# Two small-head attentions in one decoder kernel: units of one pair of heads instead of four heads, key tiles weighed in twos, a second copy of the queries, masked columns left out, and one in eight of the maxima taken by ScalarE and GpSimd

## The chip, the cores and the metric

The kernel runs on one core of a Trainium2 chip. The metric is the device time of one execution in microseconds (us). The engines are TensorE (PE, its weight loads PEld), VectorE (DVE), ScalarE (ACT), GpSimd (POOL) and SyncE (SP), which here only starts DMA transfers.

## What is computed

Two decoder layers over x of 1024 tokens by 128, with a context of 6404 by 96. All is float32. The change touches the first two of the six blocks:

```
x = x + self_attention(layernorm(x))             # L0: 16 heads of 8, causal, 1024 queries and keys
x = x + cross_attention(layernorm(x), ctx_768)   # L0: 16 heads of 8, 1024 queries, 6404 keys
x = x + mixture_of_experts(layernorm(x))         # L0
x = x + attention_over_heads(layernorm(x))       # L1, per token, 16 by 16
x = x + cross_attention(layernorm(x), ctx_768)   # L1: 16 heads of 64, 6404 keys
x = x + mixture_of_experts(layernorm(x))         # L1

scores = einsum('bhqd,bhkd->bhqk', q, k) / sqrt(8);  scores = where(causal, scores, -inf)   # self only
probs = softmax(scores, axis=-1);  out = einsum('bhqk,bhkd->bhqd', probs, v)
```

## The kernel before, in words

`decoder` runs the blocks one after another; a barrier of all engines stands between two of them. For the two small-head attentions it calls `project_small_heads` and then `attend_small_heads`.

The projection makes q and k of all heads (`fills` of 512 columns), splits each float32 value into three bfloat16 parts (ACT takes the first and second part, DVE the rest and the third) and writes the parts to DRAM through a ring of three (`RING`, semaphores `out`, L198 waits for it). After the fills, TensorE makes the values, four tiles of 128 keys to a PSUM bank, and DVE copies them into `Vall` (L222).

The attention loads from DRAM so that a head's score is one bfloat16 product over 64 rows: six row blocks of 8 hold the six products of parts that matter (`PRODUCTS`, `ROWS`), and one row (`ROW`) is one in the keys and minus the query's maximum in the queries. Two heads (s = 0, 1) lie side by side, on rows 0 to 63 and 64 to 127. A group is four heads: two such pairs, a = 0, 1.

Work goes in units n of one group by one half of the queries (512): 8 units for each attention (`UNITS`). In a unit there is

- a maximum item ("m") for each chunk of 512 keys, pair and tile of 128 queries. TensorE makes the scores query by key in two PSUM banks, one for each head (`take`, L421; on the diagonal it adds a mask, L427), and DVE reduces each bank to 128 maxima (L544). Cross-attention: 13 chunks x 2 pairs x 4 tiles = 104 items and 208 reductions in a unit.
- after a unit's last item, one reduction over chunks (L548), a turn ("t") of the maxima to rows: 16 products of one column with the identity for each pair (L438), and ACT's `negate`, which writes minus the maxima into the row `ROW` of `Qst` (L506).
- steps j, one for each tile of 128 keys (51 in a cross unit, 4 or 8 in a self unit): `score(j, 0)` and `score(j, 1)` on banks 0 to 3 (L460; with the causal mask over all 512 columns, L465), ACT's exponentials of 128 x 1024 (L525), and `weigh(j)`: four products side by side in column groups of 32, one for each head, into bank 4 (L479).
- ACT copies the sums out (L513), TensorE turns them ("o", L445), DVE divides (L556, L560).

The order is written down before the kernel is built (`plan`): the maxima of unit n+1 are spread over the steps of unit n, and `AHEAD` items (4 self, 10 cross) beyond it. TensorE's order in step j is: the two scores, the first half of the step's items, `weigh(j-1)`, the second half. Items take their banks in turn from three, 5 to 7 (`bank`), two banks each: so an item waits (L398) until the item before it has had its first bank reduced, and the item before that its second. No step starts before all items of unit 0 and `AHEAD` more are through (`first`), on the same three banks.

SP loads all parts. From group 2 on it waits until the group two before is scored. The query tile is single in `Qst`, and the row for minus the maxima stands in it: before the maxima of group g+1 POOL must clear that row again (L372, `row_cleared`), which comes after `spare` in POOL's order. `spare` is `clear_cross` during the self attention: POOL clears the tiles of the later cross attention (L1539, L1542, L1543) and sets their ones rows (L1534).

Of the kernel before, what the change touches and what calls it, by code (L numbers as in the profile page):

```python
# [19 lines left out]
P = 128  # L20
# [16 lines left out]
ROWS = (0, 8, 16, 24, 40, 48)  # L37
ROW = 32
# [99 lines left out]
def project_small_heads(nc, name, m, PS, keysT, krows, nkeys, wk, wv, qsrcT, wq, bq, kparts, qparts, Vall,  # L138
                        spare=None):
# [3 lines left out]
    ntiles = -(-nkeys // P)  # L143
    RING = 3
    fills = [("q", f * HALF, HALF) for f in range(HALVES)]
    fills += [("k", c, min(HALF, ntiles * P - c)) for c in range(0, ntiles * P, HALF)]
    with ExitStack() as stack:
        s = Mem(nc, stack, name)
        rest = s.sb("rest", [P, 2, HALF])
        parts = s.sb("parts", [P, RING, PARTS, HALF], BF16)  # L150
        biased = s.sb("biased", [P, 2, HALF])
        filled, biased_ok, part1, rest1 = s.sem("filled"), s.sem("biased_ok"), s.sem("part1"), s.sem("rest1")
        part2, part3 = s.sem("part2"), s.sem("part3")
        out = [s.sem(f"out{b}") for b in range(RING)]
        v_filled, v_copied, ones_set = s.sem("v_filled"), s.sem("v_copied"), s.sem("ones_set")
        vbanks = -(-ntiles // 4)
        block = stack.enter_context(nc.Block())

        @block.tensor
        def _(pe):  # L160
            for n, (kind, c, w) in enumerate(fills):
                if n >= 2:
                    pe.wait_ge(rest1, n - 1)
                if kind == "q":
                    i = pe.matmul(PS[:, n % 2, 0:w], wq, qsrcT[0:P, c:c + w], start=True, stop=True)
                else:
                    i = pe.matmul(PS[:, n % 2, 0:w], wk, keysT[0:krows, c:c + w], start=True, stop=True)
                i.then_inc(filled, 1)
            for t in range(ntiles):
                b = t // 4  # L170
                if t % 4 == 0 and b >= 4:
                    pe.wait_ge(v_copied, b - 3)
                i = pe.matmul(PS[:, 4 + b % 4, (t % 4) * P:(t % 4 + 1) * P], keysT[0:krows, t * P:(t + 1) * P], wv,
                              start=True, stop=True)
                if t % 4 == 3 or t == ntiles - 1:
                    i.then_inc(v_filled, 1)

        @block.scalar
        def _(act):
            def second(n):  # L180
                w = fills[n][2]
# [1533 lines left out]
```

## Time and profile before

| | |
|---|---|
| time, median of 3 runs | 4343.45 us (4342.44 to 4351.64) |
| the profiled execution | 4342.88 us, its span 4341.1 us |
| PE busy | 3724.0 us (86%) |
| DVE busy | 2818.0 us (65%) |
| ACT busy | 1998.2 us (46%) |
| POOL busy | 1868.0 us (43%) |
| self attention, first item to last division | 44.66 to 298.0 us |
| cross-attention, first item to last division | 382.78 to 1601.9 us |

PE busy is the sum over the whole program. The two attentions of the change are the first 1602 us; the blocks after them, from 1602 us on, are not touched. A row of the timeline gives start, length, engine, line, operation, the tiles, and in brackets the idle time before it and what ended it. Rows of the same kind that follow each other closely are one row with xN; consecutive instructions of an engine can overlap, so the length of such a row is less than the sum.

### The profile page before, as it was taken

How to read it: one execution, taken by the hardware profiler on the slowest of the kernel's cores; microseconds unless marked ns; L12 is line 12 of the kernel's file. 1: busy time of each engine (PE TensorE's matmuls, PEld its weight loads, DVE VectorE, ACT ScalarE, POOL GpSimd, SP SyncE). 2: the span in 40 equal slices, each digit the busy share in tenths (PEclk: the TensorE clock that was granted, in tenths of full speed). 3: DMA queues.
4: the chain of work that ended last, by engine and by line, in shares of the span. 5: the costliest groups of instructions: out<-in, count | busy, mean ns of one | idle time of the engine just before them, and what ended most of it. 6: DMA issues, size and time to landing. Idle time of an engine off the chain costs nothing. (4 is left out here: it accounts for less than half of the span.)

```text
span 4341.1 us, 56316 instructions
## 1 busy us (share of the span) xinstructions
PE 3724.0 (86%) x21560; PEld 1506.4 (35%) x21560; DVE 2818.0 (65%) x4320; ACT 1998.2 (46%) x2265; POOL 1868.0 (43%) x760
## 2 busy tenths in 40 slices
PE   5775478888888889885899999999999999999799
PEld 1222112221122224332344444444444444444343
DVE  4436899999999702276666676666667666675222
ACT  2441067777777872250244444444444444444312
POOL 3500000000000000050488887888888788889700
PEclk7885599999999988795899999999999999999889
DMA  2004000200100000060011010101101010011110
GB/s 62 15 1 107 0 1 1 28 1 1 28 1 1 1 18 25 6 247 11 15 28 29 25 30 27 29 27 29 29 25 31 28 29 27 27 29 32 34 41 5
DMA packets 71842, 122.88 MB, mean 28 GB/s; under 512 B 9741, under 2 KB 25691, under 8 KB 70907
## 3 DMA queue, kind: packets, MB, share of 16 engines
q1 hardware_dynamic: 71580, 119.28, 9.8%
q8 instruction: 177, 2.90, 0.3%
q14 instruction: 85, 0.70, 0.1%
HBM read 84.62 MB, written 34.64 MB: 27 GB/s over the span
## 5 line engine op out<-in xcount | busy, mean ns | idle before, releaser
L967 POOL TENSOR_TENSOR att_total<-att_total,att_prob 128x1024 f32<-128x1024 f32 x608 | 1569.9, 2582 | 333.9 <-ACT att_prob L1162 282.3
L1179 DVE TENSOR_REDUCE att_top_piece<-PS 128x1 f32<-128x512 f32 (+1 forms) x1664 | 1036.7, 665 | 364.4 <-PE PS L1028 354.5
L544 DVE TENSOR_REDUCE att_top_piece<-PS 128x1 f32<-128x512 f32 (+4 forms) x1856 | 1128.5, 654 | 217.2 <-PE PS L421 107.0
L1162 ACT ACTIVATE att_prob<-PS 128x1024 f32<-128x1024 f32 x816 | 791.6, 1022 | 1005.6 <-PE PS L1086 1001.8
L525 ACT ACTIVATE att_prob<-PS 128x1024 f32<-128x1024 f32 x912 | 880.4, 1021 | 358.1 <-PE PS L460 293.9
L1099 PE MATMUL PS<-att_prob,att_vals 128*64 128x512 f32 x3264 | 791.9, 605 | 3.7 <-issue 2.9
L421 PE MATMUL PS<-cross_Kstack,cross_Qstack 64*128 64x512 bf16 (+1 forms) x1664 | 343.2, 403 | 275.0 <-DVE att_top_piece L544 255.7
L1028 PE MATMUL PS<-att_k_hi,att_q_hi 64*128 64x512 f32 (+1 forms) x1664 | 396.7, 469 | 87.1 <-DVE att_top_piece L1179 86.5
L361 POOL COPY cross_Vst<-cross_Vall 128x1836 f32<-128x1836 f32 x4 | 7.6, 1898 | 1036.4 <-PE PS L479 989.9
L479 PE MATMUL PS<-att_prob,cross_Vst 128*32 128x512 f32 x3264 | 437.9, 605 | 0.6 <-ACT att_prob L525 0.4
L421 PEld LDWEIGHTS PS<-cross_Kstack,cross_Qstack 64*128 64x128 bf16 x1664 | 94.9, 94 | 785.1 <-DVE att_top_piece L544 749.9
L1073 PE MATMUL PS<-att_q_hi,att_k_hi 64*128 64x512 f32 x1632 | 327.9, 397 | 1.1 <-ACT att_prob L1162 1.1
L1028 PEld LDWEIGHTS PS<-att_k_hi,att_q_hi 64*128 64x128 f32 x1664 | 167.4, 190 | 463.4 <-issue 273.9
L1073 PE MATMUL PS<-att_q_hi,att_k_lo 64*128 64x512 f32 x1632 | 323.5, 391 | 0.0
L1073 PE MATMUL PS<-att_q_lo,att_k_hi 64*128 64x512 f32 x1632 | 323.0, 390 | 0.0
L1099 PEld LDWEIGHTS PS<-att_prob,att_vals 128*64 128x64 f32 x3264 | 197.5, 136 | 335.8 <-issue 328.7
L460 PE MATMUL PS<-cross_Qstack,cross_Kstack 64*128 64x512 bf16 x1632 | 256.0, 379 | 11.1 <-ACT att_prob L525 6.6
L1229 DVE TENSOR_TENSOR k_xn<-k_xn,att_prob 128x1024 f32<-128x1024 f32 x160 | 209.5, 1309 | 58.4 <-ACT att_prob L1162 58.4
L1086 PE MATMUL PS<-att_minus_max,att_key_ones 32*128 32x512 f32 x1632 | 207.1, 496 | 0.0
L1196 DVE TENSOR_TENSOR att_k_lo<-PS,att_k_hi 128x512 fp32r<-128x512 f32 (+1 forms) x104 | 70.8, 681 | 206.8 <-ACT att_k_hi L1144 206.8
L1073 PEld LDWEIGHTS PS<-att_q_hi,att_k_hi 64*128 64x128 f32 x1632 | 155.2, 185 | 47.6 <-ACT att_prob L1162 23.1
L1073 PEld LDWEIGHTS PS<-att_q_hi,att_k_lo 64*128 64x128 f32 x1632 | 155.1, 185 | 34.9
(240 smaller groups left out, 2870.5 us busy)
## 6 DMA issues: line engine op xcount, KB each, us to landing
att_vals<-values SPq DMA_DIRECT2D x192, 256.0 KB, 2.6
values<-mla_stage SPq DMA_DIRECT2D x24, 1024.0 KB, 4.1
f_w<-in_f_w SPq DMA_DIRECT2D x40, 256.0 KB, 4.5
cross_Kstack<-kparts SPq DMA_DIRECT2D x36, 204.0 KB
kparts<-proj_parts SPq DMA_DIRECT2D x42, 128.0 KB
att_vals<-values SPq DMA_DIRECT2D x16, 192.0 KB, 2.3
k_ctxT<-in_ctxT SPq DMA_DIRECT2D x1, 2448.0 KB
cross_Kstack<-kparts SPq DMA_DIRECT2D x36, 64.0 KB
```

Of the source, the lines that this page charges most:

```text
L421: i = pe.matmul(PS[:, bank(p + s), 0:w], Qst[rows, g % 2, a, at:at + P], Kst[rows, g % 2, a, c * HALF:c * HALF + w], start=True, stop=True ...
L460: i = pe.matmul(PS[:, 2 * (e % 2) + s, :], Kst[rows, g % 2, a, kt * P:(kt + 1) * P], Qst[rows, g % 2, a, cols(n)], start=True, stop=not ma ...
L479: i = pe.matmul(PS[32 * k:32 * k + 32, PV, :], Vst[:, kt, k, :], prob[:, j % RING, k, :], start=(kt == 0), stop=(kt == tiles_of(n) - 1), t ...
L525: act.activation(prob[:, j % RING, 2 * a:2 * a + 2, :].rearrange("p a b -> p (a b)"), PSf[:, e % 2 * 2 * HALF:(e % 2 * 2 + 2) * HALF], ACT ...
L544: dve.tensor_reduce(top_piece[:, n % 2, k, c:c + 1], PS[:, bank(p + s), 0:w], AX, ALU.max).then_inc(dve_freed, 1)
L967: pool.tensor_tensor(so_far, so_far, prob[0:rows, j % RING, :, :], ALU.add).then_inc(summed, 1)
L1028: ins = pe.matmul(PS[:, bank(at + s), 0:w], q_hi[strip(s), n % QBUFS, qt * P:(qt + 1) * P], k_hi[strip(s), p % 2, c * HALF:c * HALF + w], ...
L1073: pe.matmul(PS[:, b + s, :], k[strip(s), p % 2, keys], q[strip(s), n % QBUFS, :], start=start, stop=False, tile_position=(s * DH2, 0))
L1099: i = pe.matmul(PS[strip(s), PV, :], vals[:, value_slot(n, kt // 4), kt % 4, strip(s)], prob[:, j % RING, s, :], start=(kt == 0), stop=(kt ...
L1162: act.activation(prob[:, j % RING, :, :].rearrange("p a b -> p (a b)"), PSf[:, b:b + 2 * HALF], ACT.Exp, scale=scale).then_inc(exped, 1)
L1179: dve.tensor_reduce(top_piece[:, n % 2, s * QT + qt, c:c + 1], PS[:, bank(at + s), 0:w], AX, ALU.max).then_inc(dve_freed, 1)
L1229: dve.tensor_tensor(total_dve, total_dve, now, ALU.add).then_inc(dve_summed, 1)
```

## The change

`project_small_heads` and `attend_small_heads` become one function, `small_heads`, with one block of engines.

- A unit is one pair of heads by one half of the queries: 16 units. A cross unit has 52 items.
- A step is two tiles of keys (26 steps in a cross unit, the last one with one tile; 2 or 4 in a self unit). `weigh` puts the two heads of the first tile in column groups 0 and 1 and of the second in 2 and 3; the two halves of the sums are added when they are turned ("o"), by a product with `fold`, two identities on top of each other.
- `ROW` stays 32, but the last two row blocks lie behind it, so that a strip is 49 rows and not 64.
- Queries are held twice: `Qm` for the maxima, whose row 32 stays zero, and `Qs` for the scores, where ACT writes minus the maxima. L372's clearing and `row_cleared` are gone; `clear_cross` is shorter and sets rows as float32 words, two bfloat16 each.
- "t" is four transposes of a 128 x 128 tile whose columns 32 and 96 hold the maxima.
- In the causal attention, scores, exponentials and `weigh` leave out the columns before the diagonal (`first_column`), and the mask is added to 128 columns (256 in one tile of every other unit), not 512.
- In the cross-attention the second bank of every item with qt = 3 (of chunks 0 to 10: 11 of a unit's 104 banks) is copied by ACT into `run` or a ring of three `stage` tiles, and POOL joins it to `run` as run + max(stage - run, 0) in three instructions. DVE reduces `run` once a unit.
- `first` uses all eight banks. The projection has rings of four, makes a values bank after each keys fill, ACT and DVE copy these by turns, and ACT starts the load of the first piece of keys while SP loads the queries.

```diff
@@ items, bank by bank @@
+    def is_copied(item, s):
+        return not causal and item[0] == "m" and s == 1 and item[3] == QT - 1 and item[2] < NCH - 2
+        need = 2 if item[0] == "m" else 1
+        if k < len(first):
+            mine = [(at + i) % 8 for i in range(need)]
+        else:
+            mine = [SIDE + (at + i) % BANKS for i in range(need)]
...
+        waits[item] = [user[b] for b in mine if b in user]
@@ weigh @@
-                for k in range(GROUP):
-                    i = pe.matmul(PS[32 * k:32 * k + 32, PV, :], Vst[:, kt, k, :], prob[:, j % RING, k, :],
-                                  start=(kt == 0), stop=(kt == tiles_of(n) - 1), tile_position=(0, 32 * k))
+                for par, kt in enumerate(kts):
+                    lo = first_column(n, kt, par, i)
+                    for s in range(2):
+                        r = 32 * (2 * par + s)
+                        ins = pe.matmul(PS[r:r + 32, PV, lo:HALF], Vst[:, u % 2, kt, s, :],
+                                        prob[:, j % RING, par, s, lo:HALF], start=(i == 0),
+                                        stop=(kt + 2 >= tiles_of(n)), tile_position=(0, r))
@@ turn of the maxima, turn of the sums @@
-                        for qt in range(QT):
-                            k = (a * QT + qt) * 2 + s
-                            i = pe.matmul(PS[r:r + 1, bank(p), qt * P:(qt + 1) * P], top[:, n % 2, k:k + 1],
-                                          ident[:, :], start=True, stop=True, tile_position=(0, r))
+                    for qt in range(QT):
+                        i = pe.transpose(PS[:, banks[item][0], qt * P:(qt + 1) * P], top[:, qt, :], ident[:, :])
...
+                        i = pe.matmul(PS[:, banks[item][0], qt * 64:(qt + 1) * 64], heads_out[:, qt * P:(qt + 1) * P],
+                                      fold, start=True, stop=True)
@@ the mask of the scores @@
-                        i = pe.matmul(PS[:, 2 * (e % 2) + s, :], identb[:, :],
-                                      by_key[:, HALF - P - first_col:2 * HALF - P - first_col], start=False, stop=True)
+                        i = pe.matmul(PS[:, 2 * (e % 2) + s, lo:diagonal + P], identb[:, :],
+                                      by_key[:, HALF - P - diagonal + lo:HALF], start=False, stop=True,
+                                      skip_group_check=True)
@@ the copied maxima: ACT, POOL, DVE @@
+                    act.activation(to, PS[:, banks[item][1], :], ACT.Copy).then_inc(tile_copied, 1)
...
+                    pool.wait_ge(tile_copied, copy_number[item] + 1)
+                    pool.wait_ge(tile_joined, i)
+                    at, now = run[:, :], stage[:, i % STAGE, :]
+                    pool.tensor_tensor(now, now, at, ALU.subtract).then_inc(tile_ahead, 1)
+                    pool.wait_ge(tile_ahead, 2 * i + 1)
+                    pool.tensor_scalar(now, now, 0.0, None, ALU.max).then_inc(tile_ahead, 1)
+                    pool.wait_ge(tile_ahead, 2 * i + 2)
+                    pool.tensor_tensor(at, at, now, ALU.add).then_inc(tile_joined, 1)
...
+                        dve.wait_ge(tile_joined, joined_up_to[n])
+                        dve.tensor_reduce(top_piece[:, n % 2, 2 * QT - 1, 0:1], run[:, :], AX,
+                                          ALU.max).then_inc(run_taken, 1)
@@ clear_cross, before @@
-                if g == 0:
-                    pool.memset(Kcross[:, :, :, :], 0.0).then_inc(cross_cleared, 1)
...
-                    ones_rows(pool, Kcross, 0, NCTX, cross_cleared)
@@ attend_small_heads, before: the row in the queries @@
-                        pool.memset(Qst[r:r + 1, (g + 1) % 2, :, :], 0.0).then_inc(row_cleared, 1)
...
-                                pe.wait_ge(row_cleared, 2 * (g - 1))
```

The first place is TensorE in the cross-attention, in the steps of the first unit. Kernel before (L460 scores, L421 item, L479 weigh):

```order
L460 MATMUL PS<-cross_Qstack,cross_Kstack 128x512 x4
L421 MATMUL PS<-cross_Kstack,cross_Qstack 128x512 x2
L479 MATMUL PS<-att_prob,cross_Vst 32x512 x4
L421 MATMUL PS<-cross_Kstack,cross_Qstack 128x512 x2
L460 MATMUL PS<-cross_Qstack,cross_Kstack 128x512 x4
L421 MATMUL PS<-cross_Kstack,cross_Qstack 128x512 x2
L479 MATMUL PS<-att_prob,cross_Vst 32x512 x4
L421 MATMUL PS<-cross_Kstack,cross_Qstack 128x512 x2
```

The same engine and place in the changed kernel (L489 scores, L450 item, L515 weigh):

```order
L489 MATMUL PS<-cross_Qscore,cross_Kstack 128x512 x4
L450 MATMUL PS<-cross_Kstack,cross_Qmax 128x512 x2
L515 MATMUL PS<-att_prob,cross_Vst 32x512 x4
L450 MATMUL PS<-cross_Kstack,cross_Qmax 128x512 x2
L489 MATMUL PS<-cross_Qscore,cross_Kstack 128x512 x4
L450 MATMUL PS<-cross_Kstack,cross_Qmax 128x512 x2
L515 MATMUL PS<-att_prob,cross_Vst 32x512 x4
L450 MATMUL PS<-cross_Kstack,cross_Qmax 128x512 x2
```

Nothing has moved inside a step: the same four kinds in the same order with the same counts.

The second place is ACT in a later cross unit of the changed kernel, about the end of one unit (L605 exponentials, L572 minus the maxima, L586 copies for POOL); before, the exponentials of a unit stood there with four L506 and one L513 among them:

```order
L605 ACTIVATE att_prob<-PS 128x1024 x4
L586 ACTIVATE att_stage<-PS 128x512
L605 ACTIVATE att_prob<-PS 128x1024 x10
L572 ACTIVATE cross_Qscore<-PS 1x512 x2
L605 ACTIVATE att_prob<-PS 128x1024 x2
L586 ACTIVATE att_run<-PS 128x512
```

A copy stands behind every fourth exponential, which is every second step, and none in four of the steps.

The third place is POOL during the self attention. Kernel before (row writes of the later cross tile and the clearing that TensorE waits for):

```order
L1534 MEMSET cross_Kstack 1x4x6404
L372 MEMSET self_Qstack 1x2048 x2
```

Changed kernel:

```order
L374 COPY self_Vst<-self_Vall 128x16x9
L1648 MEMSET cross_Kstack 1x4x3202
L1648 MEMSET cross_Kstack 1x4x62
L374 COPY self_Vst<-self_Vall 128x16x9
```

The clearing behind the long write is gone, and the write has half the elements.

## Rows read from the trace of the kernel before

**Rows 1.** Windows: length, busy time (instructions) of each engine, PEclk, DMA share, GB/s.
```profile
44.60:298.80 254.20, 192.23 (x1312) 59.47 (x1312) 103.53 (x216) 116.32 (x136) 72.87 (x12) 0.86 0.03 10
690.90:962.90 272.00, 224.91 (x1714) 55.38 (x1712) 258.86 (x423) 203.61 (x215) 5.50 (x3) 1.00 0.08 12
2150.00:4000.00 1850.00, 1806.17 (x10970) 848.99 (x10970) 1253.05 (x1885) 807.12 (x884) 1531.12 (x603) 1.00 0.10 28
```

**Rows 2.** Timeline, one step in the middle of the cross-attention.
```profile
903.68 0.39 PE L421 MATMUL PS<-cross_Kstack,cross_Qstack 64*128 64x512 bf16 x2 [0.45 <-DVE att_top_piece L544]
904.00 1.06 PE L479 MATMUL PS<-att_prob,cross_Vst 128*32 128x512 f32 x8
905.00 0.39 PE L421 MATMUL PS<-cross_Kstack,cross_Qstack 64*128 64x512 bf16 x2
905.65 1.94 ACT L525 ACTIVATE att_prob<-PS 128x1024 f32<-128x1024 f32 x2 [0.65 <-PE PS L460]
906.27 0.39 PE L421 MATMUL PS<-cross_Kstack,cross_Qstack 64*128 64x512 bf16 x2 [0.45 <-DVE att_top_piece L544]
```

**Rows 3.** Groups by line and form, 540 to 1508 us: busy, mean ns, idle before.
```profile
L544 DVE TENSOR_REDUCE att_top_piece<-PS 128x1 f32<-128x512 f32 x1343 | 858.1, 686 | 29.9 <-PE PS L421 18.7
```

**Rows 4.** Timeline, two items one step apart where the last chunk has 260 keys.
```profile
805.61 0.29 PE L421 MATMUL PS<-cross_Kstack,cross_Qstack 64*128 64x260 bf16 x2
...
807.72 0.29 PE L421 MATMUL PS<-cross_Kstack,cross_Qstack 64*128 64x260 bf16 x2
```

**Rows 5.** Timeline, the stretch before the first step of the cross-attention.
```profile
382.78 0.61 PE L421 MATMUL PS<-cross_Kstack,cross_Qstack 64*128 64x512 bf16 x2 [16.35 <-DMA cross_Kstack<-kparts]
...
417.61 1.29 DVE L544 TENSOR_REDUCE att_top_piece<-PS 128x1 f32<-128x512 f32 x2 [0.20 <-PE PS L421]
...
552.39 1.94 ACT L525 ACTIVATE att_prob<-PS 128x1024 f32<-128x1024 f32 x2 [12.58 <-PE PS L460]
```

**Rows 6.** Timeline of ACT and TensorE at unit ends; then the copies one unit apart.
```profile
675.95 2.03 PE L438 MATMUL PS<-k_ident,att_top 128*1 128x128 f32 x29
...
690.91 0.60 ACT L513 ACTIVATE att_heads_out<-PS 128x512 f32<-128x512 f32 x1
...
826.89 0.60 ACT L513 ACTIVATE att_heads_out<-PS 128x512 f32<-128x512 f32 x1
```

**Rows 7.** Timeline, two steps of the last cross unit, and the end.
```profile
1593.56 1.06 PE L479 MATMUL PS<-att_prob,cross_Vst 128*32 128x512 f32 x8
...
1595.40 1.07 PE L479 MATMUL PS<-att_prob,cross_Vst 128*32 128x512 f32 x8
...
1602.91 1.64 PE L586 MATMUL PS<-k_ident,k_O 128*128 128x128 f32 x8 [1.59 <-PEq L55]
```

**Rows 8.** Timeline, the first loads of the cross-attention.
```profile
367.78 4.75 SPq L382 DMA_DIRECT2D cross_Qstack<-qparts  x12
```

**Rows 9.** Timeline, POOL and TensorE in the self attention, two places.
```profile
134.28 21.44 POOL L1534 MEMSET cross_Kstack<- 1x25616 bf16 x1
...
159.64 0.29 PE L421 MATMUL PS<-self_Kstack,self_Qstack 64*128 64x128 bf16 x2 [17.32 <-issue]
...
220.53 0.29 PE L421 MATMUL PS<-self_Kstack,self_Qstack 64*128 64x128 bf16 x2 [8.27 <-issue]
```

**Rows 10.** Timeline, turn of the sums and the two masks in the self attention.
```profile
171.15 0.29 PE L427 MATMUL PS<-self_by_query,k_identb 128*128 128x128 bf16 x2
...
173.53 0.66 PE L445 MATMUL PS<-k_ident,att_heads_out 128*128 128x128 f32 x4
...
176.52 0.60 PE L465 MATMUL PS<-self_by_key,k_identb 128*128 128x512 bf16 x2
```

**Rows 11.** Groups by form: POOL over the whole span.
```profile
L951 POOL TENSOR_TENSOR k_O<-k_O,att_sums 128x512 f32<-128x512 f32 x16 | 21.5, 1347 | 6.3 <-DVE att_sums L1209 6.3
L361 POOL COPY cross_Vst<-cross_Vall 128x1836 f32<-128x1836 f32 x4 | 7.6, 1898 | 1036.4 <-PE PS L479 989.9 <-POOLq L55 46.5
```

**Rows 12.** Groups by form, 2150 to 4000 us.
```profile
L1179 DVE TENSOR_REDUCE att_top_piece<-PS 128x1 f32<-128x512 f32 x1387 | 892.1, 685 | 284.5 <-PE PS L1028 275.2
```

More of the change, by code:

```diff
@@ L375, in _ @@
[L375 to L391 removed]
+            pool.memset(Vall[:, 0:NT, :, DH:DH + 1], 1.0).then_inc(v_ones, 1)
@@ new lines, in _ @@
+            pool.wait_ge(v_ones, 3 if nkeys % P else 1)
+            pool.wait_ge(v_by_act, VBANKS // 2)
+            pool.wait_ge(v_by_dve, VBANKS - VBANKS // 2)
+            for u in range(2):
+                stage_values(u)
+            for item in first:
+                join(item)
+            for j in range(STEPS):
+                n, i = steps[j][0], j - base[steps[j][0]]
+                for item in plan[j]:
+                    join(item)
+                u = n // HALVES
+                if n % HALVES == 0 and i == 1 and 1 <= u and u + 1 < PAIRS:
+                    stage_values(u + 1)
+                    if spare is not None:
+                        pool.wait_ge(staged, u + 2)
+                        spare(pool, u)
@@ L403, in take @@
                 if item[0] == "m":
[L404 to L414 removed]
+                    c, qt, w = item[2:]
@@ L485, in _ @@
             for j in range(STEPS):
-                score(j, 0)
-                score(j, 1)
+                for par in range(len(steps[j][1])):
+                    score(j, par)
                 items = plan[j]
@@ new lines, in _, with side @@
+            second(len(fills) - 1)
+            for n in range(HALVES, min(len(fills), HALVES + PIECE)):
+                act.wait_ge(out[n % OUT], 16 * PARTS * (n // OUT + 1))
+            load(act, Kst, kparts, 0, piece(0), 0, first_loaded[0])
+            def side(item):
+                if item[0] == "t":
+                    n = item[1]
+                    g, a = place(n)
+                    act.wait_ge(top_turned, n + 1)
+                    for s in range(2):
+                        r = 64 * s + ROW
+                        act.activation(Qs[r:r + 1, g % 2, a, cols(n)], PS[r:r + 1, banks[item][0], :], ACT.Copy,
+                                       scale=-1.0).then_inc(negated, 1)
+                elif item in copy_number:
+                    n, c = item[1:3]
+                    act.wait_ge(max_scored, maximum_number[item] + 1)
+                    if c == 0:
+                        if n >= 1:
+                            act.wait_ge(run_taken, n)
+                        to = run[:, :]
+                    else:
+                        i = join_number[item]
+                        if i >= STAGE:
+                            act.wait_ge(tile_joined, i - STAGE + 1)
+                        to = stage[:, i % STAGE, :]
+                    act.activation(to, PS[:, banks[item][1], :], ACT.Copy).then_inc(tile_copied, 1)
```

686 lines of the change are left out of this document (360 added, 326 removed).

## The prediction

> **What bounds the kernel now.** Both attentions of the change lie in the first 1602 us; nothing after them is touched, so the sum is made over this stretch. I read the windows first, to see which engine is full, then the timeline of one step, to see which wait ends last in it, then the stretches before the first step and after the last.
>
> In the middle of the cross-attention no engine is full: of 272.0 us TensorE is busy 224.9, DVE 258.9, ACT 203.6, at a granted clock of 1.00, which is 2.4 GHz [rows 1]. DVE at 95% looks like the bound. The step says something else. Steps follow each other in 906.27 - 903.68 = 2.59 us [rows 2]. Two reductions of one item take 1.29 us as a row, so the second starts 1.29 - 0.69 = 0.60 after the first [rows 3, 5]; four at that spacing are 2.40 us, less than 2.59. The path that closes on itself is this one [rows 2, 3]: item a issues (903.68), `weigh` 0.32 later (904.00), item b 1.00 later, when `weigh` has streamed (905.00), b's products end 0.39 later (905.39), DVE reduces b's first bank in 0.69 (906.08), and the next a, which needs just that bank, issues at 906.27. The 0.19 left over are two handovers. 0.32 + 1.00 + 0.39 + 0.69 + 0.19 = 2.59. The second bank of an item is not on it. Where the items are 260 keys wide the same path gives 807.72 - 805.61 = 2.11 us [rows 4].
>
> A unit of 51 steps takes 826.89 - 690.91 = 136.0 us [rows 6]; 47 x 2.59 + 4 x 2.11 = 130.2 of it are steps, 5.8 are the turns at its end (the 32 turn products are two runs like that of 2.03 us in rows 6, and one run of 0.66 for the sums, rows 10, with what waits behind them).
>
> Before the first step stand 104 items and ten of the lead on three banks, at half the clock (an item's products 0.61, not 0.39): DVE waits 0.20 for TensorE at each, 1.49 us an item; 552.39 - 382.78 = 169.6 us pass from the first item to the first exponential [rows 5]. The last unit has no maxima and goes at 1595.40 - 1593.56 = 1.84 us a step, near ACT's two exponentials of 1.94 as one row [rows 2, 7]; less the 1.00 of `weigh` that leaves 0.84 for two scores.
>
> In the self attention TensorE is busy 192 of 254.2 us at a clock of 0.86 [rows 1]. In two places it stands 17.3 and 8.3 us with nothing that the profile names [rows 9]; there it waits for POOL's clearing of row 32, which is queued behind a write of 21.4 us.
>
> **The change, part by part.**
>
> *Cross, before the first step.* 52 items on eight banks. DVE no longer waits 0.20: 41 items of two reductions at 1.20 (spacing 0.60) to 1.29, I take 1.25; 11 of one at 0.65; the run tile 0.65; four of these items are narrow, -1.5: 58 us. The turn at half clock and the reduction over chunks: 2. Then ten items of the lead, two with one reduction only: 12, since the scores need the banks of the last three items. 1 for handovers. 73 us against 169.6: **-97** (bounds -87, if each of 52 items keeps the 0.20, to -103).
>
> *Cross, the steps.* TensorE's order inside a step is the same as before (the first pair of order lists), and an item still waits for the first bank of the item before. The banks taken off DVE are second banks, which are not on the path. So a wide step keeps 2.59, a narrow one 2.11: 24 x 2.59 + 2 x 2.11 = 66.4 us a unit. At its end are one turn of four transposes (I take the 0.66 of four transposes in rows 10 for it) in place of two runs of 2.0, and one of the sums; each also shifts the banks by one, so that the next item waits for a second bank too, 0.6. Two times 0.66, half of the two 0.6, ACT's two row writes: 2.0, between 1.3 and the 2.9 of half of 5.8. 68.4 us a unit, where half a unit before was 68.0: nothing won.
> ACT gets 11 copies of 0.60 a unit [rows 6]: 1.94 + 0.60 = 2.54 in every second step, below 2.59 and just covered; if that cover went, a step of 2.6 to 2.8 would cost up to 2 us a unit.
> POOL gets ten joins a unit. The two-input instruction of this size is 1.35 [rows 11]; a one-input one lies between 1.90 x 512 / 1836 = 0.53 (the copy) and 1.35. A join is 3.2 to 4.1, with handovers 3.5 to 4.4, in two steps of 5.18 us: covered. DVE waits for the last join only five items (three steps) after its tile: covered too. Both at nothing.
> Units 0 to 13: 14 x 68.4 = 958, with 2.5 for the first, which starts at the low clock (552.39 to 690.91 is 138.5 before). Unit 14 has only 42 items left to take: 16 steps of 2.59 and 10 of some 2.2 (two scores 0.84, `weigh` 1.0, one item 0.3): 64. Unit 15 has none: 51 tiles x 0.92 = 47. The end 3 as now. Together 1075, against 1602.91 - 552.39 = 1050.5: **+24**. That a half unit in which DVE idles is replaced by one in which it works takes back a quarter of what the start gives.
>
> *Cross, projection and first loads.* SP's query load (4.75 us to issue) and the first keys after it now start on two queues at once: -4 of the 15.0 us from 367.78 to the first item [rows 5, 8]. The values between the fills, a ring of four and one barrier less: at least -1, at most -14 (the 13 value banks now come after the fills). Together -5 to -18; I take **-12**.
>
> *Self attention.* The two gaps go: 17.3 + 8.3 = 25.6 [rows 9]; `staged` is then all that TensorE needs of POOL, and its long write is half as many elements (some 10.7 us by 21.4 / 2, if the cost goes by elements) with a pair of units of over 20 us to hide in; cover gone, it would cost some of those 25.6. The mask over 512 columns, 0.53 to 0.60 for a pair of products, becomes one over 128, 0.22 to 0.29 [rows 10]: 64 x 0.32 = 20. Sixteen turns of 0.66 for sixteen runs of 2.0, minus eight more turns of sums at 0.66: 16 x 1.35 - 5 = 16. Left-out columns (a quarter of `weigh` and scores on the diagonal tiles, 0.2 each on 32 pairs): 6. Four items fewer in `first` on eight banks: 5; the smaller last unit: 3. Sum 75.6; since part of mask and columns lies beside the reductions that an item waits for (four items to a step where the next unit is the long one), I take two thirds of 20 + 6: 67. Loads on two queues and one barrier less: 5. **-72**, bounds -45 (only the gaps, the turns and a little) and -90.
>
> Sum: -97 + 24 - 12 - 72 = -157. 4342.9 - 157 = 4186, and the profiled execution is 0.6 us under the median: **4186 us**.
>
> **A rule against this change.** The reductions cost 685 ns with POOL busy 1531 of 1850 us, and 686 ns where POOL idles [rows 1, 3, 12]: no contention to be seen. The Trainium skill (Perfetto Trace Analysis, Optimizing Scalar/DVE Operations) warns that GpSimd and DVE share an SBUF read port, so that moving work between the two might not help; it also says, in SBUF — State Buffer, Who interferes with whom, that `tensor_reduce` on trn2 never contends. By the first sentence the joins would slow the reductions, by the second and by the rows they would not; the rows decide.
>
> **Rivals.**
> 1. *DVE is the bound in the steps, and the copies relieve it.* For it: 95% busy. Then two steps have seven reductions in place of eight; TensorE's own work, 0.84 + 1.00 + two items of 0.32 and at least 0.21 (512 columns at 2.4 GHz), 2.37 to 2.48 a step, comes next: 24 x 2.39 + 2 x 2.11 + 2 = 63.6, with its waits 64.4, a unit 4 shorter. 14 x 4 = 56 less: 4130 us. Against it: the path above has 2.59 with nothing left for it.
> 2. *ACT or POOL becomes the bound in the steps*, ACT through its copies behind two exponentials, or POOL with 1.9 us an instruction: two steps become 6.0, 11 x 0.8 = 9 a unit, +140: 4326 us. For it: ACT's cover is only 0.05. Against it: rows 11, and score banks for two exponentials ahead.
> 3. *Slower: the joins block DVE.* POOL's 4 us of SBUF work in every two steps would hold the reductions. The point from which the change loses is 157 / (11 x 16) = 0.9 us in two steps; if blocked for all of it, two steps take some 8.8, +3.6 x 176 = 630: over 4800 us. Against it: rows 3 and 12.
> 4. *The self attention gives only its low bound* and the start of the projection too: 4186 + 27 + 7 = 4220 us.
>
> **How the numbers follow.** My forecast 0.60; the first rival 0.18; the second 0.07; the third 0.03; the fourth 0.12. The range: below, the first rival with another 20 from self and projection, 4110; above, the fourth with 2 us more in each of 15 units, 4250. Slower than before by over 0.2% (8.7 us, which is about what a measurement can tell) is only the third, 0.03; within 0.2% 0.02; faster 0.95.
>
> **What would show it.** The first exponential of the cross-attention some 73 us after its first item. Copies out of the sums 68.4 us apart, and steps of 2.59 with TensorE still waiting 0.4 for DVE's first bank; if they are 64 apart, the path was not the bound; if TensorE or ACT waits there for POOL, the second rival. The reductions still 0.69 each; at 1 us or more, the third. No gap over 3 us on TensorE in the self attention, and that stage some 185 us from its first item. What would make the forecast wrong most: a step whose path is no longer through b's first bank, because ACT's copies delay the exponentials by more than the 0.05.

## The result, and the profile after

The changed kernel takes 4201.2 us (median of 4 runs, 4196.86 to 4204.58), the kernel before 4342.94 us (4 runs, 4340.66 to 4351.64). The ratio is 0.967, with a 95% interval of 0.965 to 0.969: 142 us faster. The forecast was 4186 us in a range of 4110 to 4250. Its mechanism in the cross-attention held, to 0.6 us a unit; the self attention gave less than half of what was forecast.

The profiled execution took 4204.58 us with a span of 4202.4 us, 138.7 us less than the span before. The stretches, with the difference from before:

| stretch | before | after | difference | predicted |
|---|---|---|---|---|
| self attention: first turn of `O` behind it, on the clock of the run | 298.8 | 268.4 | -30.4 | -72 |
| projection and loads, to the first cross item | 84.0 | 62.9 | -21.1 | -12 |
| cross, first item to first exponential | 169.6 | 66.9 | -102.7 | -97 |
| cross, first exponential to the first turn of `O` | 1050.5 | 1068.7 | +18.2 | +24 |
| all later blocks | 2738.2 | 2735.5 | -2.7 | 0 |

The timeline of the changed kernel has the edges of the cross-attention. Columns are start, length, engine, line, operation, tiles, idle before and who ended it; these rows answer to [rows 5, 7]:

```profile
331.30 1.89 PE L450 MATMUL PS<-cross_Kstack,cross_Qmax 49*128 49x512 bf16 x8 [18.86 <-DMA cross_Qmax<-qparts]
...
398.20 1.02 ACT L605 ACTIVATE att_prob<-PS 128x1024 f32<-128x1024 f32 x1 [4.27 <-PE PS L489]
...
1466.93 1.48 PE L696 MATMUL PS<-k_ident,k_O 128*128 128x128 f32 x8 [1.51 <-PEq L58]
```

A step in the middle of the cross-attention, which answers to [rows 2]:

```profile
703.20 1.06 PE L515 MATMUL PS<-att_prob,cross_Vst 128*32 128x512 f32 x8
...
704.20 0.39 PE L450 MATMUL PS<-cross_Kstack,cross_Qmax 49*128 49x512 bf16 x2
...
704.63 0.60 ACT L586 ACTIVATE att_stage<-PS 128x512 f32<-128x512 f32 x1 [0.44 <-PE PS L450]
705.12 1.94 ACT L605 ACTIVATE att_prob<-PS 128x1024 f32<-128x1024 f32 x2
705.30 1.27 POOL L382 TENSOR_TENSOR att_stage<-att_stage,att_run 128x512 f32<-128x512 f32 x1 [0.98 <-ACT att_stage L586]
...
705.47 0.39 PE L450 MATMUL PS<-cross_Kstack,cross_Qmax 49*128 49x512 bf16 x2 [0.45 <-DVE att_top_piece L647]
...
705.79 1.07 PE L515 MATMUL PS<-att_prob,cross_Vst 128*32 128x512 f32 x8
...
706.66 1.48 POOL L384 TENSOR_SCALAR att_stage<-att_stage 128x512 f32<-128x512 f32 x1
```

From `weigh` at 703.20 to `weigh` at 705.79 are 2.59 us, as before, and TensorE still stands 0.45 us before item a for DVE, although in this step ACT copies a bank (704.63) and POOL joins it. The copies of the sums, which answer to [rows 6]:

```profile
469.37 0.60 ACT L592 ACTIVATE att_heads_out<-PS 128x512 f32<-128x512 f32 x1
...
537.07 0.60 ACT L592 ACTIVATE att_heads_out<-PS 128x512 f32<-128x512 f32 x1
...
604.78 0.60 ACT L592 ACTIVATE att_heads_out<-PS 128x512 f32<-128x512 f32 x1
```

67.7 us a unit here and 67.8 in the later ones; half a unit before was 68.0. The windows of the changed kernel (length, busy time and instructions of PE, PEld, DVE, ACT and POOL, granted clock, DMA share, GB/s) answer to [rows 1]:

```profile
43.20:267.00 223.80, 186.74 (x1216) 73.33 (x1216) 106.53 (x239) 101.50 (x144) 33.17 (x13) 0.74 0.06 17
...
147.00:155.00 8.00, 5.40 (x42) 1.98 (x42) 6.27 (x12) 3.52 (x6) 3.92 (x3) 0.89 0.00 0
155.00:163.00 8.00, 7.26 (x42) 3.19 (x38) 3.40 (x9) 2.63 (x4) 0.00 (x0) 0.50 0.01 2
...
537.10:604.80 67.70, 57.24 (x424) 14.21 (x422) 59.02 (x98) 56.23 (x66) 41.34 (x31) 1.00 0.00 1
```

In the cross-attention the clock is 1.00 as before. In the self attention it is 0.74, where it was 0.86, and it is here that the forecast failed. Groups by form over 469 to 1350 us answer to [rows 3, 11]; the copies and the joins are there for the first time:

```profile
L647 DVE TENSOR_REDUCE att_top_piece<-PS 128x1 f32<-128x512 f32 x1106 | 716.5, 686 | 105.1 <-PE PS L450 94.8
...
L384 POOL TENSOR_SCALAR att_stage<-att_stage 128x512 f32<-128x512 f32 x130 | 192.9, 1484 | 11.4
L386 POOL TENSOR_TENSOR att_run<-att_run,att_stage 128x512 f32<-128x512 f32 x130 | 166.0, 1277 | 10.9
L382 POOL TENSOR_TENSOR att_stage<-att_stage,att_run 128x512 f32<-128x512 f32 x130 | 165.7, 1275 | 328.3 <-ACT att_stage L586 328.3
L586 ACT ACTIVATE att_stage<-PS 128x512 f32<-128x512 f32 x130 | 77.6, 597 | 45.4 <-PE PS L450 45.4
```

The reductions took 686 ns while POOL worked 41.3 of 67.7 us beside them. That agrees with the Trainium skill (SBUF — State Buffer, Who interferes with whom), by which `tensor_reduce` on trn2 never contends with GpSimd. These reductions read PSUM; the one in each unit that reads `run` in SBUF took 675 ns.

### The profile page after: what moved, and what is told of

Read it like the earlier page. It is cut to its first block and busy times, and to the rows that moved or that the text cites. A ratio compares the mean times of both kernels' runs of the same rounds, so it can differ in the third digit from the quotient of the medians.

```text
span 4202.4 us, 57008 instructions
## 1 busy us (share of the span) xinstructions
PE 3694.7 (88%) x21368; PEld 1514.6 (36%) x21368; DVE 2718.1 (65%) x4201; ACT 2076.1 (49%) x2464; POOL 2452.6 (58%) x1245
## 5 line engine op out<-in xcount | busy, mean ns | idle before, releaser
L1272 ACT ACTIVATE att_prob<-PS 128x1024 f32<-128x1024 f32 x816 | 791.6, 1022 | 1004.5 <-PE PS L1196 1000.7
L647 DVE TENSOR_REDUCE att_top_piece<-PS 128x1 f32<-128x512 f32 (+4 forms) x1680 | 1020.5, 650 | 237.3 <-PE PS L450 141.7
L605 ACT ACTIVATE att_prob<-PS 128x1024 f32<-128x1024 f32 (+2 forms) x912 | 863.8, 1004 | 188.3 <-PE PS L489 151.8
L450 PE MATMUL PS<-cross_Kstack,cross_Qmax 49*128 49x512 bf16 (+1 forms) x1664 | 330.2, 391 | 187.8 <-DVE att_top_piece L647 165.8
L515 PE MATMUL PS<-att_prob,cross_Vst 128*32 128x512 f32 x3264 | 443.7, 606 | 0.5 <-ACT att_prob L605 0.2
L382 POOL TENSOR_TENSOR att_stage<-att_stage,att_run 128x512 f32<-128x512 f32 x160 | 203.8, 1274 | 401.1 <-ACT att_stage L586 399.8
L450 PEld LDWEIGHTS PS<-cross_Kstack,cross_Qmax 49*128 49x128 bf16 x1664 | 92.8, 93 | 686.7 <-DVE att_top_piece L647 517.3
L489 PE MATMUL PS<-cross_Qscore,cross_Kstack 49*128 49x512 bf16 x1632 | 258.4, 380 | 19.5 <-ACT att_prob L605 13.2
L384 POOL TENSOR_SCALAR att_stage<-att_stage 128x512 f32<-128x512 f32 x160 | 237.4, 1484 | 14.0
L386 POOL TENSOR_TENSOR att_run<-att_run,att_stage 128x512 f32<-128x512 f32 x160 | 204.1, 1276 | 13.4
```

What stands on the lines that cost most here:

```text
L384: pool.tensor_scalar(now, now, 0.0, None, ALU.max).then_inc(tile_ahead, 1)
L450: i = pe.matmul(PS[:, banks[item][s], 0:w], Qm[rows, g % 2, a, at:at + P], Kst[rows, g % 2, a, c * HALF:c * HALF + w], start=True, stop=Tr ...
L489: i = pe.matmul(PS[:, 2 * (e % 2) + s, lo:HALF], Kst[rows, g % 2, a, kt * P:(kt + 1) * P], Qs[rows, g % 2, a, n % HALVES * HALF + lo:(n % ...
L515: ins = pe.matmul(PS[r:r + 32, PV, lo:HALF], Vst[:, u % 2, kt, s, :], prob[:, j % RING, par, s, lo:HALF], start=(i == 0), stop=(kt + 2 >= ...
L605: act.activation(prob[:, j % RING, par, :, lo:HALF], PS[:, 2 * (e % 2):2 * (e % 2) + 2, lo:HALF], ACT.Exp, scale=scale).then_inc(exped, 1)
L647: dve.tensor_reduce(top_piece[:, n % 2, s * QT + qt, c:c + 1], PS[:, banks[item][s], 0:w], AX, ALU.max).then_inc(dve_freed, 1)
```

## The experiments

Unit times below are distances of two copies of the sums; kernel times are medians of four runs.

**1. No copies.** `is_copied` gives False, and DVE's reduction of `run` goes.

```diff
-        return not causal and item[0] == "m" and s == 1 and item[3] == QT - 1 and item[2] < NCH - 2
+        return False
```

> DVE takes all maxima of the cross-attention itself; ACT's 12 copies and POOL's 11 joins of a unit go. By the path theory the banks given away are second banks and off the path: copies of the sums stay 67.8 us apart, only the stretch before the first exponential grows, by 11 reductions of 0.6, 66.9 -> 73 us; kernel 4201 -> 4205 to 4212 us. By the rival (DVE is the bound, the copies relieve it) a unit grows by some 4 us, kernel some 4260 us. If the copies only cost, it is a little faster than 4201.

Measured: 4214.1 us (ratio to before 0.970, 0.969 to 0.972), 2 us above the expected range. Units of 67.7 us in the middle; first item 333.35, first exponential 407.42, so 74.1 us in place of 66.9. DVE is busy 64.8 us of a unit, not 59.0, and the unit is no longer. The copies pay only ahead of the first step.

**2. Half of the first bank, or half of the second.** Both relieve DVE by the same amount.

```diff
-dve.tensor_reduce(..., PS[:, banks[item][s], 0:w], AX,
+dve.tensor_reduce(..., PS[:, banks[item][s], 0:(HALF // 2 if not causal and s == 0 and w == HALF else w)], AX,
```

(`s == 1` for the second bank. Both kernels leave keys out of the maxima.)

> In the cross-attention DVE reduces only the left 256 columns of the first bank of each wide item (the right half of these keys is left out of the maxima). By the path theory (item a, weigh, item b, DVE's first bank, next a) a step loses about half of the 0.69 us reduction, some 0.3 us, until TensorE's own 2.0 us or ACT's 1.9 us a step are near: step 2.59 -> 2.3 to 2.4, copies of the sums 67.8 -> 60 to 62.5 us apart, kernel 4201 -> about 4100 to 4125 us. If DVE's total (59.0 of 67.7 us a unit) were the bound, the gain would be the same here and in the kernel with the second banks halved.

> The same cut of 256 columns, but in the second bank of each wide item (the right half of these keys is left out of its maxima). DVE is relieved as much as with the first banks halved. By the path theory nothing comes of it: copies of the sums stay 67.8 us apart, kernel 4201 us within 8. If DVE's total were the bound, the unit would fall to 60 to 63 us and the kernel to some 4110 us.

Measured: first bank 4108.4 us (0.946, 0.945 to 0.948), second bank 4198.2 us (0.967, 0.965 to 0.968). The timeline of the kernel with half a first bank, then of the one with half a second:

```profile
523.27 0.61 ACT L592 ACTIVATE att_heads_out<-PS 128x512 f32<-128x512 f32 x1
...
585.10 0.61 ACT L592 ACTIVATE att_heads_out<-PS 128x512 f32<-128x512 f32 x1
```

```profile
532.44 0.60 ACT L592 ACTIVATE att_heads_out<-PS 128x512 f32<-128x512 f32 x1
...
599.78 0.60 ACT L592 ACTIVATE att_heads_out<-PS 128x512 f32<-128x512 f32 x1
```

61.8 us a unit against 67.3; the changed kernel takes 67.7 there. The halved reduction takes 425 ns in place of 686; 24 wide steps by 0.26 are 6.3 us a unit, and 5.9 came. The second banks gave 0.3 to 0.4 for the same relief. The step goes through b's first bank, and DVE's total is not its bound.

**3. Single waits, and another order.** In the cross-attention each of an item's two products waits for its own bank and tells DVE of itself; then the items are also laid around the scores. The edit is shortened:

```diff
-                for before in waits[item]:
-                    wait_freed(*before)
+                        if not causal and banks[item][s] in user_before[item]:
+                            wait_freed(*user_before[item][banks[item][s]])
@@ second kernel: order in a cross step @@
-                score, score, item a, weigh, item b
+                score, a's first product, score, a's second and b's first, weigh, b's second
```

> In the cross-attention each of an item's two products waits for its own bank alone and tells DVE of itself, in place of one wait and one signal for both; order unchanged. By the path theory the product whose bank is free goes earlier, and DVE starts on b's first bank before the second product ends: 0.05 to 0.1 us a step, 20 to 40 us of the kernel, 4161 to 4181 us. Rival: the two products then no longer stream side by side (each half of TensorE's rows), an item takes 0.43 us longer and the twice as many waits cost some 0.05 each: 4201 to 4240 us.

> As the kernel with single waits, and the order on TensorE inside a cross step is changed too: score, first product of item a, score, a's second product and b's first, weigh, b's second product; before, score, score, item a, weigh, item b. By the path theory three of the four banks of a step are then refilled while weigh waits or runs, and DVE never waits for the end of weigh with more than one bank empty: step 2.59 -> 2.40 to 2.48 us, unit 67.8 -> 63 to 65, kernel 4140 to 4165 us. Rival: the scores are parted by products that wait for DVE, so the second exponential is late, ACT becomes part of the path, and the step grows to 2.6 to 2.9: 4200 to 4320 us.

Measured: 4173.9 us (0.961, 0.960 to 0.962) with units of 65.5 us, and 4158.0 us (0.957, 0.956 to 0.959) with units of 64.8. Both beat the changed kernel. With the spread order TensorE is busy 62.7 of 64.8 us:

```profile
529.10:593.90 64.80, 62.69 (x424) 15.02 (x422) 57.31 (x98) 56.45 (x66) 41.36 (x32) 1.00 0.01 1
```

The same 424 products had taken 57.2 us. In its timeline one product stands where the pair had stood, and is as long as the pair (0.39 us in the step above):

```profile
699.66 0.39 PE L454 MATMUL PS<-cross_Kstack,cross_Qmax 49*128 49x512 bf16 x1
...
700.97 0.39 PE L454 MATMUL PS<-cross_Kstack,cross_Qmax 49*128 49x512 bf16 x1
```

So a part of the won wait seems to be spent again on products that no longer stream side by side. This is a reading of the busy records, whose ends are modelled; no run tests it by itself.

**4. The mask over all columns.** In the self attention only.

```diff
-                        i = pe.matmul(PS[:, 2 * (e % 2) + s, lo:diagonal + P], identb[:, :],
-                                      by_key[:, HALF - P - diagonal + lo:HALF], start=False, stop=True,
+                        i = pe.matmul(PS[:, 2 * (e % 2) + s, lo:HALF], identb[:, :],
+                                      by_key[:, HALF - P - diagonal + lo:2 * HALF - P - diagonal], start=False, stop=True,
```

> In the self attention the mask product of a score runs again to column 512 in place of 128 columns; the result is the same. It adds 64 times some 0.3 us of TensorE work at full clock where the scores begin left of the diagonal's end. Theory 1: the narrow masks won less than their work because TensorE's clock in this stage is granted at 0.74 only, and more work raises it: self stage 223.8 us within 5, clock above 0.74. Theory 2: the work is simply on the path: the stage grows by 10 to 20 us at the same clock, kernel 4212 to 4220 us.

Measured: 4211.8 us (0.970, 0.969 to 0.972). From the first item to the last copy of the sums 228.5 us against 221.9, +6.6, at a clock of 0.77 against 0.74. This lies between the two theories. The edit also adds less than the 64 times 0.3 us of its expectation: the columns left of `lo` stay out, so a masked tile gets 192 more columns on average and not 384. At full clock two units are busy 19.6 us on TensorE in place of 18.3 (rows under experiment 5), an estimated 10 us in the eight pairs of the stage, and 6.6 came.

**5. The self attention's items twice.** The same two products are issued again into the same banks.

> In the self attention each item's two products are issued twice into the same banks (result unchanged): 15 us more of TensorE work at 2.4 GHz, 31 us at 1.2 GHz. Theory 1 (the low clock is what the stage lost, and it comes from TensorE being too little busy): granted clock 0.74 -> 0.85 or more, the stage 223.8 us -> 205 to 225 though work was added. Theory 2 (clock does not follow work, or the added work is on the path): 235 to 255 us at a clock near 0.74.

Measured: 4216.7 us (0.972, 0.969 to 0.974). The stage takes 224.2 us against 221.9, with 192 more products (1400 instructions for 1208) but not more time on TensorE:

```profile
42.49:266.70 224.21, 187.22 (x1400) 69.55 (x1400) 106.52 (x238) 100.56 (x143) 33.20 (x13) 0.84 0.06 17
```

The mean clock is 0.84 for 0.74, and busy time 187.2 for 185.7 us. This near draw is made of two effects, which the single units tell apart. Pairs of units (by copies of the sums at 124.42, 148.60, 172.78 and 196.96) take 24.2 us each here, at a clock of 1.00; the two pairs behind them take 29.2 and 28.5 us, at 0.77 and 0.70. In the changed kernel two units take 24.2 us in some places and 27.2 in others:

```profile
97.41 0.60 ACT L592 ACTIVATE att_heads_out<-PS 128x512 f32<-128x512 f32 x1 [0.90 <-PE PS L515]
...
124.60 0.60 ACT L592 ACTIVATE att_heads_out<-PS 128x512 f32<-128x512 f32 x1 [0.90 <-PE PS L515]
...
148.78 0.60 ACT L592 ACTIVATE att_heads_out<-PS 128x512 f32<-128x512 f32 x1 [0.90 <-PE PS L515]
...
175.94 0.60 ACT L592 ACTIVATE att_heads_out<-PS 128x512 f32<-128x512 f32 x1 [0.90 <-PE PS L515]
```

No pair of the changed kernel has the full clock. One pair of the kernel with spread parts has it, and that kernel's self attention is the changed kernel's. The windows of pairs of units, first of the changed kernel, then of the one with spread parts (at full clock, and the pair behind):

```profile
97.41:124.60 27.19, 23.72 (x153) 9.75 (x153) 13.43 (x31) 12.72 (x19) 11.38 (x3) 0.75 0.05 15
124.60:148.78 24.18, 20.36 (x153) 7.96 (x153) 13.36 (x31) 12.68 (x19) 11.38 (x3) 0.86 0.11 33
```

```profile
93.40:115.69 22.29, 18.30 (x153) 7.80 (x153) 13.34 (x31) 12.63 (x18) 11.38 (x3) 1.00 0.07 18
115.69:142.71 27.02, 23.55 (x153) 9.40 (x153) 13.44 (x31) 12.73 (x19) 11.38 (x3) 0.75 0.10 30
```

At full clock, a pair with wide masks and a pair with items twice:

```profile
205.61:229.07 23.46, 19.57 (x153) 7.80 (x153) 13.33 (x31) 12.62 (x18) 0.32 (x1) 1.00 0.01 1
```

```profile
148.60:172.78 24.18, 20.20 (x177) 8.18 (x177) 13.37 (x31) 12.62 (x19) 3.92 (x3) 1.00 0.07 20
```

Two things follow. At the same clock, TensorE's work is on the path: 1.3 us more busy made the pair 1.2 us longer, and 1.9 us more made it 1.9 longer. And the clock is worth more than either: the same products take 22.3 us at 1.00, 24.2 at 0.86 and 27.2 at 0.75.

**6. The kernel before, with POOL's clearing ahead of its long write.**

```diff
-                if spare is not None:
-                    pool.wait_ge(staged, g + 1)
-                    spare(pool, g)
                 if 2 <= g + 1 < GROUPS:
                     ...                                   # the clearing of row 32
+                if spare is not None:
+                    pool.wait_ge(staged, g + 1)
+                    spare(pool, g)
```

> The kernel before, with one change: POOL clears row 32 of the next group ahead of its long write for the padded values, not behind it. The gaps of 17.3 and 8.3 us of TensorE in the self attention go: 25.6 us less, and up to 10 more if the low clock behind the gaps goes with them: 4343 -> 4307 to 4317 us, cross-attention unchanged. Rival: another wait of TensorE for POOL's queue takes their place, 4335 to 4343 us.

Measured: 4315.2 us (0.994, 0.993 to 0.995), 26.3 us less. From the first item to the last copy of the sums 226.2 us in place of 251.4, near the 25.6 of the two gaps [rows 9]. That sum hides two parts. Behind the first copy of the sums the stage is 29.8 us shorter, the gaps and 4 us of the low clock that had followed them; ahead of it the same work takes 59.3 us in place of 54.6, at a clock of 0.61 for 0.70, which rose later in this execution. Three of its copies of the sums:

```profile
154.15 0.60 ACT L513 ACTIVATE att_heads_out<-PS 128x512 f32<-128x512 f32 x1
...
180.44 0.60 ACT L513 ACTIVATE att_heads_out<-PS 128x512 f32<-128x512 f32 x1 [1.54 <-PE PS L479]
...
205.23 0.60 ACT L513 ACTIVATE att_heads_out<-PS 128x512 f32<-128x512 f32 x1
```

A unit of four heads by one half of the queries, which is as much work as two new units' average, takes 24.8 to 26.3 us here, and 25.1 on average where the clock is 1.00:

```profile
180.44:230.59 50.15, 43.79 (x330) 14.30 (x328) 25.83 (x55) 28.94 (x34) 25.49 (x4) 1.00 0.03 8
```

At that clock two new units take 22.3 us, with TensorE busy 18.3 for 21.9: the savings of masks, columns and turns are worth 2.8 us a pair, an estimated 22 us in the stage. At the clock that the changed kernel was granted it takes 24.2 to 27.2, and most or all of that is gone.

**7. Two items in every step.** The changed kernel's planner takes four items in each of the two steps of a short self unit and one in each of the four steps of a long one. This is how TensorE goes in a short unit of the changed kernel:

```profile
150.88 0.39 PE L450 MATMUL PS<-self_Kstack,self_Qmax 49*128 49x512 bf16 x2 [0.88 <-DVE att_top_piece L647]
...
153.07 0.28 PE L450 MATMUL PS<-self_Kstack,self_Qmax 49*128 49x256 bf16 x2 [0.47 <-DVE att_top_piece L647]
153.29 0.39 PE L456 MATMUL PS<-self_by_query,self_identb 128*128 128x128 bf16 x2
153.62 1.94 PE L515 MATMUL PS<-att_prob,self_Vst 128*32 128x512 f32 x8
```

One item after another waits for DVE's reductions; then the clock falls to half, and a `weigh`, 1.06 us at full clock, takes 1.94. The edit, on top of the kernel with spread parts (whose self attention is that of the changed kernel):

```diff
     def lead(n):
-        return min(12, 4 + 4 * n) if causal else 10
+        return (4 if n == 0 else 12 if n % 2 == 0 else 8) if causal else 10
```

> The kernel with single waits and spread parts, and in the self attention the items that TensorE takes in a step are spread evenly: two in each of the six steps of a long and a short unit, where the planner now gives four to each of the two steps of a short unit and one to each of the four steps of a long one. Theory: the low clock and the lost time of this stage come from that unevenness: in the long unit TensorE stands waiting for exponentials with one item to do and the clock falls behind it, in the short one each of four items waits 1.27 us for DVE's reductions. Then two units take 18 to 21 us in place of 24.2 or 27.2, the granted clock of the stage rises from 0.75 to 0.9 or more, the stage (first item to last copy of the sums, 219.4 us in that kernel) falls to 175 to 195 us, and the kernel to 4158 - 35 = 4115 to 4135 us. Rival: the clock stays near 0.75 whatever the order, because the work itself is too little; the stage then falls by 10 us at most, 4148 us or more.

Measured: 4113.5 us (0.948, 0.947 to 0.950), 44.5 less than the kernel it stands on (4158.0); the kernel before, run beside each, was 4.4 us faster beside this one, so by the ratios it is 40. The stage went from 219.4 to 174.5 us. Time and stage are just below the expected ranges. The windows of the kernel with even items:

```profile
41.84:216.30 174.46, 155.48 (x1208) 63.29 (x1208) 105.62 (x238) 99.84 (x144) 33.19 (x13) 0.89 0.08 22
83.00:219.00 136.00, 126.89 (x1068) 54.15 (x1066) 81.74 (x190) 89.50 (x129) 33.19 (x13) 1.00 0.07 19
```

```profile
129.00 0.60 ACT L616 ACTIVATE att_heads_out<-PS 128x512 f32<-128x512 f32 x1
...
147.84 0.60 ACT L616 ACTIVATE att_heads_out<-PS 128x512 f32<-128x512 f32 x1
```

The same 1208 products, and from 83 us on the clock is granted in full. Two units take 18.8 us in place of 24.2 to 27.2. Of the 45 us, an estimated 21 are the evenness itself: six pairs of units behind the start, 3.5 us each, by 22.3 us at full clock in the uneven order (TensorE idle 4.0 of them) and 18.8 in the even one (idle 0.7). The other 24 are put down to the clock, which no longer falls.

**8. Queries loaded ahead of the wait for the last key writes.** On top of the last one.

```diff
-            wait_out(sp)
+            for b in range(2):
+                sp.wait_ge(out[b], 16 * PARTS)
             load(sp, Qm, qparts, 0, slice(0, T), 1, qm_loaded[0])
+            wait_out(sp)
```

> As the kernel with even items, and SP issues the load of the queries for the maxima ahead of its wait for the last key writes, not behind it. In the changed kernel the first item of the cross-attention waited 18.9 us for that load, issued at 325.12 after the wait, the last write at 318.5; ACT's load of the first keys had been issued from 314.78 on. Theory: the first item of the cross-attention comes 5 to 7 us earlier, kernel 5 to 8 us below the one with even items. Rival: the loads share the DMA engines with the last writes, and only 0 to 2 us are won.

Measured: 4109.4 us (0.947, 0.946 to 0.949), 4.0 less, under the 5 to 8 expected. The first item of the self attention comes 1.9 us earlier (39.99 for 41.84), and the stretch from the last self exponential to the first cross item is 67.3 us for 69.5, 2.2 less. TensorE still waits 17.3 us there for that same load, so what holds it is not only the place of its issue. The rival of the expectation, that the load shares the DMA engines with the last writes, is not ruled out: their busy share was 0.90 from 266 to 270 us, about its issue at 269.5. This is the fastest version that was run, some 90 us below the changed kernel.

**9. That version without the copies.**

> The kernel with even items and early queries, but DVE takes all maxima of the cross-attention (no copies by ACT, no joins by POOL). In the changed kernel that made no difference to a unit (67.7 to 67.8 us), since the step waited for the first bank. Here a unit is 64.8 us, and DVE without the copies is busy 64.8 us a unit: theory: now the copies are needed, a unit grows to 66.5 to 68 us, the start by 7: kernel 4109 + 15 x 2.5 + 7 = 4140 to 4165 us. Rival: the copies are still worth nothing in the steps, kernel 4116 us.

Measured: 4131.5 us (0.952, 0.951 to 0.954). Units of 65.7 us for 64.8, and from the first item (282.35) to the first exponential (356.39) 74.0 us for 66.9. The time is below the expected 4140 to 4165. DVE is busy 63.1 of 65.6 us:

```profile
490.90:556.50 65.60, 61.87 (x424) 15.66 (x422) 63.09 (x108) 51.12 (x54) 1.05 (x1) 1.00 0.00 1
```

The copies, worth nothing in a step of 2.59 us, are worth 0.9 us a unit once the step is shorter: less than the 1.7 or more expected.

## Why the prediction was right, and where it was not

- **The path of a cross step** (a, `weigh`, b, DVE's first bank): right. The step kept 2.59 us, the unit came to 67.7 for 68.4 forecast, and experiments 1 and 2 tell it from the first rival, DVE as the bound: only first banks count. The end of a unit was priced 0.6 us too high, 13 times, 8 us; the last two units took 64.7 and 48.4 us, 2.1 more than forecast. That is the 6 us between +24 and +18.
- **Copies and joins at no cost**: right. A join takes 1.28 + 1.48 + 1.28 = 4.04 us, at the upper end of the 3.2 to 4.1 forecast (the one-input instruction above its bound of 1.35, the two-input ones below theirs), and fits two steps of 5.18. Neither the second nor the third rival showed up.
- **The start of the cross-attention**: right, 66.9 us for 73. Eight banks took the wait of 0.20 us away; the copies' share of it is 7.2 us by experiment 1.
- **Projection and loads**: -21 for -12, beyond the -18 of the bounds. No run takes its parts apart. TensorE still waits 18.9 us for the queries.
- **Self attention**: the term that failed, -72 forecast, bounds -45 and -90, measured -30. The gaps were sized well: 25.6 forecast, 25.1 by experiment 6 over the whole stage. The first exponential comes 12.4 us after the first item (55.57 - 43.16), before 22.4 (67.11 - 44.66): another 10. These two are more than the 29.4 us by which the stage got shorter up to its last copy of the sums, so what lies behind them became some 6 us slower in sum. The failed step is the 16 of the turns and "two thirds of 20 + 6", with no term for the clock beside them: work taken off TensorE was counted as time at a clock that stays. Two things were wrong in it. The size: at full clock the savings are worth 2.8 us a pair of units (experiment 6), an estimated 22 us and not 33. And the clock, which was the larger: it fell from 0.86 to 0.74 over the stage. The changed kernel's five pairs of units from 97.41 to 227.31 took 27.2 us three times and 24.2 twice, some 18 us more than at full clock, and the unit before them 18.8 us where the kernel with spread parts took 14.9 at a higher clock, another 4. In the short units each item waits for DVE's reductions, and the clock falls around there; experiment 7 takes most of these waits away with the same products, and the clock stays. (The fourth rival named the right term, but its -45 was still too much.)

In the profiled execution the forecast was 18 us too low: 42 in the self attention, less 9, 6 and 6 in the three other stretches and 3 in the blocks that were not touched. By the median it was 15. So the total came close partly by luck: one miss of 42 us stood against 24 us of gains that were not forecast. Of the signs named, two failed: the stage of some 185 us took 222 to its last copy of the sums, and one wait on TensorE in it, ahead of the first step, is over 3 us (3.7, for DVE).

Some things stay open. The 22.3 us at full clock rest on one pair of units in one run; the pairs with added work, 23.5 and 24.2 us, fit it. Why the clock falls in one short unit and not in the next is not shown, only that it does and what it costs. The low clock at the start of the stage (0.50 over the first 35 us in the changed kernel, 0.70 over the first 55 before) was not priced. And the turns and the left-out columns were not undone by themselves; only half of the mask was.

## What to carry to other kernels

Work taken off an engine gives time only where the path of the step goes through it: follow one step until it closes on itself, and do that in every stage, not only in the longest. When items are planned by unit, look at how many fall into each step; two in every step beat four, four, one, one, one, one, by 3.5 of 22.3 us at the same clock, because each engine's wait is then covered by another's work. And when TensorE's work shrinks in a stage with waits, read the granted clock of that stage's windows before counting the gain. Compare units at the same clock, too: over a whole stage, work that costs time and a clock that gives it back can look like work that costs nothing.

## What the runs showed of the hardware

- POOL's one-input `TENSOR_SCALAR` (maximum with 0, 128x512 float32) took 1484 ns, longer than its two-input `TENSOR_TENSOR` of the same size, 1275 ns. The prediction had taken the two-input one as the upper bound.
- POOL's write of one row went by elements, not by bytes: 21.44 us for 25,616 bfloat16 [rows 9], 10.76 us for 12,808 float32 words, the same bytes (11.12 with the short second write behind them).
- TensorE's granted clock fell to 0.50 (1.2 GHz) behind a stretch in which it had worked 5.4 of 8 us. The same 153 TensorE instructions of two units took 22.3 us at a mean clock of 1.00, 24.2 at 0.86 and 27.2 at 0.75. With 192 added products the mean over the stage was 0.84 in place of 0.74: 1400 instructions were busy 187.2 us, 1208 had been busy 185.7.
- Pairs of 128x512 products on two halves of the rows, 0.39 us a pair, showed more busy time when each product waited for its own bank: 57.2 us in a unit became 61.7, and 62.7 in the spread order.
